# Twelve instead of ten sequences sorted in the second feed-forward, and finished tiles scattered to their tokens

## The reference

```
x = x + 0.5 * ffn(layernorm(x))
x = x + attention(layernorm(x))      # 16 heads of 8, keys = queries = centred x
x = x + 0.5 * ffn(layernorm(x))
ffn: logits = x Wg + bg; the 2 best of 8 experts, gates normalised to sum 1
     h = relu(x W1[e] + b1[e]) (128 -> 256);  y = h W2[e] + b2[e] (256 -> 128)
     out = sum over the 2 experts of gate * y
```

## Time and profile before

| | us |
|---|---|
| three runs | 1040.12, 1041.96, 1043.07 |
| the profiled execution | 1034.83 |
| its span, first to last instruction | 1033.0 |
| PE, DVE, ACT, POOL busy in it | 995.5, 810.4, 848.6, 511.1 |

### The profile page before, as it was taken

One profiled execution on the slowest core, in us unless ns is written; L12 is line 12 of the kernel. 1 busy time (PEld: TensorE's weight loads), 2 busy tenths in 40 slices (PEclk: granted clock), 3 DMA queues, 4 the chain that ended last, 5 costly groups with the idle time before them and its releaser, 6 DMA issues.

```text
span 1033.0 us, 20557 instructions
## 1 busy us (share of the span) xinstructions
PE 995.5 (96%) x6626; PEld 569.4 (55%) x6626; DVE 810.4 (78%) x2226; ACT 848.6 (82%) x1240; POOL 511.1 (49%) x602
## 2 busy tenths in 40 slices
PE   7999999999999999999999999999999999999996
PEld 5677777533332588833233333333328887777775
DVE  6899999867667677757778778777638876999898
ACT  4655553699999999889999999999998997666654
POOL 5546777744344100035776767775311000688775
PEclk8999999999999999999999999999999999999999
DMA  5533223000051244310111111112413462343442
GB/s 187 186 128 134 103 101 105 14 18 20 19 161 47 75 143 145 112 57 30 37 37 37 37 38 34 40 37 79 132 56 130 127 236 91 119 144 139 149 158 83
DMA packets 58894, 96.19 MB, mean 93 GB/s; under 512 B 8699, under 2 KB 29987, under 8 KB 58787
## 3 DMA queue, kind: packets, MB, share of 16 engines
q1 hardware_dynamic: 47664, 73.63, 21.3%
q0 software_dynamic: 9728, 19.94, 6.4%
q10 hardware_dynamic: 1396, 1.30, 0.4%
HBM read 58.46 MB, written 36.39 MB: 92 GB/s over the span
## 4 chain that ended last, share of the span: by engine, by line
PE 56%; ACT 20%; issue 11%; DVE 8%; DMA 2%; POOL 1%; SPq 0%; ACTq 0%; DVEq 0%; POOLq 0%
ACT probs L1922 13%; PE ps L1696 9%; ACT sums L1922 6%; PE ps L1681 5%; PE ps L677 3%; PE ps L693 3%; PE ps L678 3%; PE ps L679 3%; PE ps L698 3%; PE ps L694 3%; DVE low L947 3%; PE ps L1314 2%; PE ps L1316 2%; PE ps L1315 2%; PE ps L1325 2%
## 5 line engine op out<-in xcount | busy, mean ns | idle before, releaser
L1922 ACT ACTIVATE probs<-ps 128x1024 f32<-128x1024 f32 x344 | 337.2, 1144 | 6.3 <-PE ps L1681 5.2
L1637 POOL DMA_INDIRECT found<-tiles,home x152 | 152.0, 1000 | 270.8 <-DMA tiles<-sums 207.0
L1625 POOL DMA_INDIRECT sorted<-xn,slot x152 | 152.3, 1002 | 125.6 <-ACT probs L1922 76.9
L1125 ACT ACTIVATE high<-ps 128x512 fp32r<-128x512 f32 x208 | 121.0, 594 | 85.9 <-PE ps L679 82.5
L1696 PE MATMUL ps<-probs,value 128*32 128x512 f32 x1376 | 183.3, 604 | 1.8 <-ACT probs L1922 1.6
L1922 ACT ACTIVATE sums<-ps 128x1024 f32<-128x1024 f32 x168 | 175.1, 1144 | 1.6 <-PE ps L1696 0.6
L1681 PE MATMUL ps<-shared 32*128 32x512 f16 x1024 | 140.9, 384 | 8.9 <-ACT probs L1922 2.4
L947 DVE SCALAR_TENSOR_TENSOR low<-ps,high 128x512 fp32r<-128x512 f32 x208 | 133.1, 681 | 10.4 <-ACT high L1125 9.8
L1201 POOL TENSOR_TENSOR sums<-sums 128x512 f32<-128x512 f32 x70 | 90.5, 1293 | 55.8 <-DVE sums L981 47.0
L1681 PEld LDWEIGHTS ps<-shared 32*128 32x128 f16 x1024 | 38.0, 91 | 136.3 <-ACT probs L1922 73.5
L693 PE MATMUL ps<-high,weights 128*128 128x512 f32 x208 | 84.0, 404 | 6.5 <-DVE sums L981 6.4
(11 more groups left out here) (202 smaller groups left out, 1871.0 us busy)
## 6 DMA issues: line engine op xcount, KB each, us to landing
probs<-gates SPq DMA_DIRECT2D x28, 512.0 KB, 3.9
found<-sorted SPq DMA_DIRECT2D x52, 256.0 KB, 2.6
tiles<-sums SPq DMA_DIRECT2D x52, 256.0 KB, 2.0
wide<-gates SPq DMA_DIRECT2D x24, 512.0 KB, 6.0
sorted<-zeros SPq DMA_DIRECT2D x16, 512.0 KB
out<-X SPq DMA_DIRECT2D x15, 256.0 KB
sorted<-xn,slot POOLq DMA_INDIRECT x152, 2.3
found<-tiles,home POOLq DMA_INDIRECT x152
```

The costliest lines, as they stand in the source:

```text
L1125: nc.scalar.activation(high[:, third(m), c, :], ps[:, hidden_bank(m, c), :], ACT.Relu).then_inc(sm["f_high"], 1)
L1625: nc.gpsimd.indirect_dma_start(sorted_rows[group_of(q)], bass.IndirectOffsetOnAxis(ap=slot[:, q % XNS, k, j:j + 1], axis=0), xn[:, rows_sl ...
L1637: nc.gpsimd.indirect_dma_start(found[:, q % 2, k, j, :], None, tile_rows[group_of(q)], bass.IndirectOffsetOnAxis(ap=home[:, q, k, j:j + 1] ...
L1922: nc.scalar.activation(ring[ring_at(n)], ps[:, score_banks(n), :], ACT.Exp, scale=SCORE).then_inc(sm["a_probs"], 1)
```

## The change

1. The second group has twelve sequences (0 to 11) instead of ten: 31 tiles instead of 27, and four whole jobs (7 to 10, sequences 12 to 15) instead of six.
2. Two sequences of the group (`STILL`, sequences 0 and 1) are routed inside the first tile stage, on all engines; the other ten during the second attention, as before.
3. Table rows are 130 numbers wide (`XW`) instead of 128: each carries the row number to which its result goes, and its gate. Both are written beside the normalised token (`route_marks`); between the sends to the first and to the second expert POOL swaps the pair of marks, after the first four sends have landed.
4. In the second tile stage DVE keeps the marks of a tile (`keep_marks`), makes the target rows (`find_homes`) and, instead of copying the finished tile, multiplies it by the gates (`weigh_out`). POOL scatters it with 4 indirect DMAs (`scatter`) into a table in token order. Tiles are no longer stored; 11 buffers (`SPREAD`) hold tiles that wait. 22 tiles are scattered in front of the last stage's work on POOL's queue, the 9 others (`LEFT`) in its first two jobs (`SCATTERS`).
5. The gathers, ACT's scalings and DVE's 20 adds of the last stage are gone. Instead, after all scatters have landed, SP loads for each sequence two plain blocks of 256 KB (`load_back`, 6 pairs of buffers), POOL adds the two (`pair_up`), DVE adds the sum to `X` (`add_pair`): 12 times, one per iteration in experts 2 to 7 of the third last-stage job and 0 to 5 of the fourth (`PAIRED`).
6. In the first two jobs of the last stage DVE makes five of the seven sums (`EARLY_ADDS`) instead of three.
7. In both attentions the logits of a routed sequence come one head group later, and `attn_means` one step later.

```diff
-NJOBS = 9, 10
+NJOBS = 9, 12
+XW = D + 2
+SPREAD = 11
+LEFT = 9
+BUFFERS = 6
+STILL = 2
+STILL_AT = 1, 8
-COLLECTS = [(2, 2, 1, 2, 2, 2, 1, 2)] * 5 + [(2, 2, 2, 2, 2, 0, 0, 0)]
-ADDED = {(0, 7): 0, (1, 0): 1, (1, 4): 2, (1, 5): 3, (2, 0): 4, (2, 1): 5, (2, 5): 6, (2, 6): 7, (3, 1): 8, (3, 2): 9,
...
+SCATTERS = (2, 2, 2, 3, 2, 2, 2, 2), (2, 2, 3, 2, 2, 3, 2, 3)
+PAIRED = {(2, 2 + k): k for k in range(6)} | {(3, k): 6 + k for k in range(6)}
+EARLY_ADDS = 1, 2, 3, 4, 5
...
+            def load_back(r):
+                if r == 0:
+                    for k in range(SPREAD):
+                        sp.wait_ge(scattered[k], scatters(k, (RETURNED - k + SPREAD - 1) // SPREAD))
+                if r >= BUFFERS:
+                    sp.wait_ge(sm["c_added"], GROUP[1] + r - BUFFERS + 1)
+                for k in range(TOPK):
+                    at = (RETURNED + k * NJOBS[1] + r) * T
+                    sp.dma_start(buffers[r % BUFFERS][:, k, :],
+                                 spread_rows[at:at + T, :].rearrange("(p j) d -> p (j d)", j=J)).then_inc(returned[r % BUFFERS], 16)
...
+                if n == WHOLE + 2:
+                    for r in range(BUFFERS):
+                        load_back(r)
...
-            return n >= WHOLE and e in (LAST_ADDS if n == JOBS - 1 else ADDS)
+            return n >= WHOLE and e in (LAST_ADDS if n == JOBS - 1 else EARLY_ADDS if n < JOBS - 2 else ADDS)
...
-                    if (n - WHOLE, e) in ADDED:
-                        at = ADDED[n - WHOLE, e]
-                        add_half(dve, GROUP[1] + at // TOPK, at % TOPK)
+                    if (n - WHOLE, e) in PAIRED:
+                        add_pair(dve, PAIRED[n - WHOLE, e])
...
-                    if n >= WHOLE:
-                        c = sum(sum(job) for job in COLLECTS[:n - WHOLE]) + sum(COLLECTS[n - WHOLE][:e])
-                        for at in range(c, c + COLLECTS[n - WHOLE][e]):
-                            collect(pool, GROUP[1] + at // (TOPK * J), at % (TOPK * J))
+                    if WHOLE <= n < WHOLE + len(SCATTERS):
+                        c = sum(sum(job) for job in SCATTERS[:n - WHOLE]) + sum(SCATTERS[n - WHOLE][:e])
+                        for at in range(c, c + SCATTERS[n - WHOLE][e]):
+                            scatter(pool, TILE0[2] - LEFT + at // J, at % J)
+                    if n >= WHOLE and (n - WHOLE, e) in PAIRED:
+                        pair_up(pool, PAIRED[n - WHOLE, e])
...
+        def pair_up(pool, r):
+
+            at = buffers[r % BUFFERS]
+            pool.wait_ge(returned[r % BUFFERS], returns(r // BUFFERS + 1))
+            nc.gpsimd.tensor_tensor(at[:, 0, :], at[:, 0, :], at[:, 1, :], ALU.add).then_inc(sm["c_paired"], 1)
+
+        def add_pair(dve, r):
+
+            s = sorted_seq(GROUP[1] + r)
+            dve.wait_ge(sm["c_paired"], r + 1)
+            nc.vector.tensor_tensor(tokens(s), tokens(s), buffers[r % BUFFERS][:, 0, :], ALU.add).then_inc(sm["c_added"], 1)
...
+            def weigh_out(t):
+                r = t - TILE0[1]
+                dve.wait_ge(sm["t_back"], t + 1)
+                if r >= SPREAD:
+                    dve.wait_ge(scattered[r % SPREAD], scatters(r % SPREAD, r // SPREAD))
...
+                nc.vector.tensor_tensor(spread[r % SPREAD], ps[:, TILE_BACK, :].rearrange("p (j d) -> p j d", j=J),
+                                        kept[:, r % KEPT, :, 1:2].to_broadcast([P, J, D]), ALU.mult).then_inc(sm["t_out"], 1)
...
+        def scatter(pool, t, j):
+
+            r = t - TILE0[1]
+            if j == 0:
+                pool.wait_ge(sm["t_out"], t + 1)
+                pool.wait_ge(sm["t_homes"], r + 1)
+            nc.gpsimd.indirect_dma_start(spread_rows, bass.IndirectOffsetOnAxis(ap=homes[:, r, j:j + 1], axis=0),
+                                         spread[r % SPREAD][:, j, :], None).then_inc(scattered[r % SPREAD], 16)
...
+                for k, q in enumerate(range(GROUP[1], GROUP[1] + STILL)):
+                    if i == STILL_AT[k]:
+                        route_stats(dve, q)
+                    if i == STILL_AT[k] + 2:
+                        route_rows(dve, q)
+                    if i == STILL_AT[k] + 3:
+                        route_copy_rows(dve, q)
...
+            for t in range(TILE0[1], TILE0[2] - LEFT):
+                for j in range(J):
+                    scatter(pool, t, j)
```

More of the change, by code:

```diff
@@ L87 @@
 INDEXED = INDEX + TILES
-NCONST = INDEXED + TILES
+TOKEN = INDEXED + TILES
+NCONST = TOKEN + J
 def constants():
@@ L296, in build @@
         value = sb("value", [P, 2, SIDES, J, G // SIDES, Q, W])
+        value_flat = value[:, :, :, :, :, :, :].rearrange("p u r j m q w -> p (u r j m q w)")
+        spread = [value_flat[:, k * T:(k + 1) * T].rearrange("p (j d) -> p j d", d=D) for k in range(SPREAD - 3)] + [
+            xn[:, k, :, 0:D] for k in range(2, 5)]
+        buffers = [found[:, k, :, :, :].rearrange("p k j d -> p k (j d)") for k in range(2)] + [
+            value_flat[:, k * TOPK * T:(k + 1) * TOPK * T].rearrange("p (k c) -> p k c", k=TOPK) for k in range(4)]
         probs = sb("probs", [P, 4, 2, T])
@@ L395, in x_loaded, with scatters, returns @@
             return x_in_sems[{0: 0, 1: 1, 2: 2, 3: 2, 4: 3, 5: 3, 6: 3, 7: 4}.get(s, 3 + s // 4)]
+        def scatters(k, tiles):
+            earlier = len(range(k, SORTED, XNS)) if k < XNS else len(range(k - XNS, NJOBS[0], 2)) if k < XNS + 2 else 0
+            return 16 * TOPK * J * earlier + 16 * J * tiles
+        def returns(times):
+            return 16 + 16 * TOPK * times
         def stream(a, b):
@@ L762, in keep_warm @@
             for _ in range(times):
-                nc.tensor.matmul(ps[:, hidden_bank(0, 0), 0:D], ones[:, :], zeros[:, :], start=True, stop=True)
+                nc.tensor.matmul(ps[:, hidden_bank(0, 0), 0:D], ones[:, :], zeros[:, 0:D], start=True, stop=True)
         def ffn_tensor(pe, first, last):
@@ L1759, in attn_tensor @@
                         route_turn(pe, job)
-                    if k == 6 and hg == 1 and job is not None:
-                        pe.wait_ge(sm["a_cent"], s + 2)
+                    if k == 6 and hg == 2 and job is not None:
+                        pe.wait_ge(sm["a_operands"], g + 2)
+                        reached(pe, sm["a_normed"], g // SIDES)
                         route_logits(pe, job)
@@ L1866, in attn_vector @@
                     route_copy_rows(dve, job)
-                if hg == 2 and job is not None:
-                    route_copy_logits(dve, job)
                 if g == 0:
@@ L2051, in _, with first_stream @@
         def _(act):
-            def nothing(i):
-                pass
+            def first_stream(i):
+                for k, q in enumerate(range(GROUP[1], GROUP[1] + STILL)):
+                    if i == STILL_AT[k] + 7:
+                        route_second(act, q)
             def second_stream(i):
@@ L2080, in _ @@
             attn_scalar(act, 0, PAUSE)
-            scalar_stream(act, 0, TILE0[1], nothing)
+            scalar_stream(act, 0, TILE0[1], first_stream)
             attn_scalar(act, PAUSE, S * G)
```

259 lines of the change are left out of this document (169 added, 90 removed).

## The result

The changed kernel took 1114.41 us (median of 4 runs, 1111.88 to 1115.88) against 1042.04 us of the kernel before: 1.0694 of it, 95% interval 1.0669 to 1.0719. The prediction said 1022, range 1003 to 1034. It was wrong: the change makes the kernel slower, and the time lies far outside the range. (One execution of the kernel before took 1806.18 us, in the sixth batch of the experiments, and is left out of the ratios.)

A forecast was written before the change was run, and what follows sets the result against it. TensorE was taken to bound both tile stages, ScalarE the second attention, and PE, DVE and POOL to be near their limit in the last stage. +3.8 + 0 + 14.7 - 39.0 - 0.5 + 1.0 = -20.0 us gave 1022, range 1003 to 1034.

The forecast's parts named there:

- forecast +3.8: First tile stage: two sequences' transposes, logits and counts on PE, 1.9 us each, all on the path; range +2 to +7.
- buffers in time: Second tile stage: 11 buffers cover POOL's slower scatters; the tightest is freed at 885 against 893, 8 us to spare.
- The chain of jobs 9 and 10: Last stage: `add_pair` waits for `pair_up`, queued behind sums; the stretch takes 102.5 us against 141.5 before; chance 0.55.
- The even iteration: Jobs 9 and 10: scale and halve 1.86 plus `add_pair` 0.6, 2.46 us, its pair having been made in time.
- A long one: Jobs 9 and 10: iteration where POOL's sum stands ahead of the pair, 6.05 us instead of 2.8 on PE; four of them.
- The pair of iteration 2: Job 9: its first `add_pair` waits 5.7 us for the load and the pair, until 954.6.
- The gain of this stretch: Last stage, first unit's end to last halve: 102.5 us instead of 141.5, a gain of 39.0.
- -38.5: Last stage: -39.0 for the stretch, -0.5 for one add fewer in the tail, +1.0 for a low clock after stalls.
- POOL's rate: Rival: 124 scatters on one queue ahead of the loads; at 1.42 us each the gain is used up; chance 0.1.
- the clock's rival: Rival: clock stays low through jobs 9 and 10, 57 us where the chain takes 48, total 1031; chance 0.08.
- the hidden chain: Rival: the chain costs nothing in jobs 9 and 10, 15 us less, total 1007; chance 0.25.
- 0.09 for slower: Whole kernel: chance that the change makes it slower, beside 0.88 for faster and 0.03 for the same.

The follow-up runs named there:

- sixth batch: The changed kernel again, 1.073 of the kernel before; and the changed kernel with three memsets ahead of each scatter of the second tile stage alone, 1100.76 us, 1.051.
- narrow_b: The changed kernel with rows of 512 bytes and scatters to each tile's own places, run again in the held condition: 1108.75 us, 1.064 of the kernel before.
- before_own: The kernel before, word for word, measured again with a profile from that chip: 1046.45 us, beside 1046.58 for the kernel before in the same batch.

## Why the prediction was wrong, by its own steps

**What held, in the free condition.** narrow_rows has the changed kernel's instructions and their order, with rows of 512 bytes and scatters to other places. Its stages, by the same cuts, against the kernel before in its free trace: first tile stage 99.6 against 96.9, +2.7 (forecast +3.8). Second attention 324.5 against 325.2 (forecast 0). Second tile stage 120.4 against 105.9, +14.5 (forecast +14.7), tiles 3.67 us apart, POOL back to back at 1.26, buffers in time. The profiled execution took 1018.2 us, forecast 1014.8; beside the kernel before of its batch the gain is 14.4 us (1034.19 to 1019.75) where 20 were forecast.

The chain of jobs 9 and 10, the step on which the forecast turned in the prediction's words, is there as worked out: DVE idle ahead of `add_pair`, released by POOL, and POOL's sum released by DVE's. From that run's timelines of DVE and of POOL:

```profile
960.18 0.69 DVE L1590 TENSOR_TENSOR X<-X,found 128x512 f32<-128x512 f32 x1 [2.89 <-POOL found L1584]
960.79 0.74 DVE L1030 SCALAR_TENSOR_TENSOR sums<-ps,b2T,wide 128x512 f32<-128x512 f32 x1
...
962.64 0.68 DVE L1007 TENSOR_TENSOR sums<-sums 128x512 f32<-128x512 f32 x1
...
966.03 1.74 DVE L1590 TENSOR_TENSOR X<-X,found 128x512 f32<-128x512 f32 x1 [2.12 <-POOL found L1584]
967.69 0.74 DVE L1030 SCALAR_TENSOR_TENSOR sums<-ps,b2T,wide 128x512 f32<-128x512 f32 x1
...
969.55 0.68 DVE L1590 TENSOR_TENSOR X<-X,value 128x512 f32<-128x512 f32 x1
970.15 0.74 DVE L1030 SCALAR_TENSOR_TENSOR sums<-ps,b2T,wide 128x512 f32<-128x512 f32 x1
```
```profile
963.47 1.30 POOL L1246 TENSOR_TENSOR sums<-sums 128x512 f32<-128x512 f32 x1 [3.33 <-DVE sums L1007]
964.72 1.28 POOL L1584 TENSOR_TENSOR found<-found 128x512 f32<-128x512 f32 x1
965.96 1.26 POOL L1584 TENSOR_TENSOR value<-value 128x512 f32<-128x512 f32 x1
```

The even iteration takes 970.15 - 967.69 = 2.46 us, exactly the forecast. A long one takes 967.69 - 960.79 = 6.90 where 6.05 was forecast (the terms written there add up to 6.03): the add took 1.74 us and not 0.69, since POOL was already at the next pair. From the first unit to the end of the last halve 102.5 us were forecast; the two rows are

```profile
896.50 0.63 PE L749 MATMUL ps<-low,weights 128*128 128x512 f32 x2
```
```profile
1005.80 1.27 DVE L998 SCALAR_TENSOR_TENSOR low<-ps,high 128x512 fp32r<-128x512 f32 x2
```

that is 1007.07 - 896.50 = 110.6 us. The pair of iteration 2 was added 63.7 us after the first unit (forecast 59.8, from 954.6 - 894.8), since SP's loads started only at 955.5; four adds of 1.75 us make 4 more. The gain of this stretch was mis-sized by 8 us, 31 instead of 39, its mechanism right.

**The step that failed.** In the second tile stage the sum has +14.7, four tiles more at 3.68 us each, with the 88 scatters beside them priced only by the time that they take on POOL's own queue; in the second attention it has 0. What these indirect DMAs do to TensorE's reports was put at nothing, without a row for it. By the profiled executions, changed kernel against kernel before:

| stretch | forecast, us | measured, us |
|---|---|---|
| ahead of the first tile stage | 0 | +5.8 |
| first tile stage | +3.8 | +4.5 |
| second attention | 0 | +22.6 |
| second tile stage | +14.7 | +74.7 |
| last stage | -38.5 | -28.2 |
| span | -20.0 | +79.4 |

The second tile stage alone makes 60 of the 99 us that the span is off, the second attention 23. (The stretch ahead of the first tile stage varies between 348 and 358 us in all traces, of both conditions.) That this is the holds, and not the work, narrow_b and narrow_rows show, one kernel in both conditions: held against free +25.6 us in the second attention, +63.0 in the second tile stage, +5 in the last stage, 96.7 over the whole span.

A second step failed with it: "The median of the runs is 1041.96, 7 us above that execution; minus 20 it gives 1022." The sum was made on one profiled execution, and the 7 us between it and the median were carried over as a constant. By before_own, in another batch, most of such a distance is the kernel before's own share of this loss, which its first trace, with no late report, does not show; and the change multiplies it.

**Why the change multiplies it.** In its second attention the kernel before has at most three indirect DMAs in a row, and in its tile stages none. Its longest rows, of four and five, stand in the last stage, which is 2 us longer in before_own. The change puts 88 scatters back to back beside the stage in which PE, ACT and DVE hand each tile on within 3.68 us, so that each hold stops all three. The clock adds to it: the granted share over the stage is 0.87, and 1.00 in the free run.

**The rivals.** The slower side was to be POOL's rate, decided at 1.42 us per scatter. Scatters came at 1.26, and the kernel was slower all the same. The rival named the right instructions, 124 on one queue, "no row shows any so dense", and priced only what they cost their own engine. No rival priced what they do to others. In the free run neither the clock's rival nor the hidden chain came about: the stretch with the chain took 110.6 us, and the granted clock of the last stage was 0.93. The 0.09 for slower was too little for a density that no row of before covered.

## What to carry to other kernels

Where a profiled execution is faster than every timed run of its kernel, it may have been taken under other circumstances: ask what the difference is made of, and whether the change grows it, before adding it as a constant. Where a change puts one kind of operation far denser than any row of the trace shows it, the unknown is its effect on the neighbours too. Beside a stage in which TensorE, ACT and DVE hand work on tightly, measure what rows of indirect DMAs from GpSimd cost: here 1.59 us from start to start ended the holds in that stage, 1.42 did not, and plain DMAs from SyncE made none. The gaps are not free: the kernel with gaps everywhere was still 3.7% slower than the kernel before, and the variant with plain DMAs does not scatter at all.

## What the runs showed of the hardware

- In the held condition rows of indirect DMAs from GpSimd, 1.26 to 1.42 us apart, make TensorE's semaphore reports late, by up to 10 us in rows of eight and twelve, while the matmuls that need no other engine run on. At 1.59 us, from 400 us on, none is late by more than 0.7. Rows of sends (first tile stage), of gathers (last stage of before_own) and of scatters all do it. ACT's, DVE's and POOL's own reports are not late, by 0.02 us at most. The row of five sends at 333 to 340 us in the changed kernel's first trace, in the first attention, is free of it, and during its like in the later traces no report is more than 0.7 us late; why was not found.
- The held condition came in five batches of six, the free one in one, and the number under which the chip is reported was the same for the free batch and a held one. What sets it stays open. The kernel before tells it: 1034 us free, 1042 to 1048 held.
- How a row of DMAs on one queue delays another engine's reports stays open as well; only its spacing was tried.
- A VectorE add of two SBUF tiles, 0.69 us alone, took 1.74 to 1.76 when GpSimd began an add of 1.26 us just before it (965.96 and 966.03 in the rows above): it ended 0.55 us after GpSimd's.
  The Trainium skill ("SBUF — State Buffer", SBUF: two separate sides) says that a VectorE operation with two SBUF inputs and a GpSimd operation that reads SBUF share a pair of ports as an exclusive lock, and that the one that starts first has it for its whole instruction. An estimate from that page: each `add_pair` beside a running pair costs up to one pair more, 1.26 us. The trace agrees within that, with 1.74 - 0.69 = 1.05 us.
